# Order of one DMA queue in a fused tower kernel: item loads ahead of the Gram stores, and the Z result stored in one DMA

## The reference

```python
h = tok(x, embeddings)
h = h + attn(layernorm(h), ...)
h = h + ffn(layernorm(h), ...)

# attn: k, q, v = short_conv(x @ W.T + b); k, q normalized per head; v = silu(v)
# b = beta * k;  v = beta * v;  then, chunk by chunk of each sequence and head:
T = jnp.tril(Bi @ KiT, k=-1)
inv = jnp.linalg.inv(eyeC + T)
Ui = inv @ (Vi - Bi @ W_t)
W_new = W_t + KiT @ Ui
...
O_i = Qi @ W_avg * a + Qi @ W_t * c + T_mat * (Qi @ KiT) @ Ui
```

## Time and profile before

| | |
|---|---|
| median of three executions | 1499.64 us |
| the profiled execution | 1499.78 us |
| its span, first to last instruction | 1498.0 us |
| TensorE clock, mean granted | 0.877 |
| first stage with items (186 to 576 us) | 390 us, DVE busy 293, PE 238 |
| DMA share in that stretch | 0.73 |
| second stage with items (576 to 800 us) | 224 us, DMA share 0.80, then 0.76 |

### The profile page before, as it was taken

How to read it: one execution, slowest core, us unless ns; L and a number is a source line. 1 busy time by engine, 2 the same in 40 slices (tenths; PEclk the granted TensorE clock), 3 DMA queues, 4 the chain that set the end, 5 groups by cost and what they waited for, 6 DMA issues and landing times. The chain is left out here.

```text
span 1498.0 us, 28824 instructions
## 1 busy us (share of the span) xinstructions
PE 1181.4 (79%) x10846; PEld 795.5 (53%) x10846; DVE 762.3 (51%) x1707; ACT 516.6 (34%) x1049; POOL 390.3 (26%) x366
## 2 busy tenths in 40 slices
PE   4855465666666564787688988999999999999997
PEld 2643344353535352566466764665566666666664
DVE  4699959586868685478547873122111121111111
ACT  3454245453636261234152323331122222222221
POOL 6100123131112021533136004661022222222222
PEclk9878778787888785578788988999999999999999
DMA  7754557768695869688687748952122232323222
GB/s 265 195 125 125 129 165 171 225 149 245 136 255 120 253 134 267 200 244 246 172 256 230 222 129 338 346 167 78 28 47 47 45 48 43 47 47 46 47 46 30
DMA packets 237366, 228.68 MB, mean 153 GB/s; under 512 B 88980, under 2 KB 177972, under 8 KB 236080
## 3 DMA queue, kind: packets, MB, share of 16 engines
q1 hardware_dynamic: 202944, 194.28, 45.8%
q0 software_dynamic: 16368, 19.96, 7.7%
q10 hardware_dynamic: 17920, 12.59, 2.8%
HBM read 117.39 MB, written 115.62 MB: 156 GB/s over the span
## 5 line engine op out<-in xcount | busy, mean ns | idle before, releaser
L1683 DVE TENSOR_TENSOR hid_all<-p_s,silu 128x512 f32<-128x512 f32 x103 | 71.2, 691 | 379.4 <-PE p_s L1534 249.7
L1733 POOL DMA_INDIRECT out_h<-y_sb,x_in x71 | 110.5, 1557 | 360.9 <-DVE y_sb L1695 338.4
L1591 ACT ACTIVATE silu<-p_m 128x512 f32<-128x512 f32 x103 | 61.6, 598 | 328.0 <-PE p_m L1527 223.3
L801 DVE SCALAR_TENSOR_TENSOR cv<-raw,conv_sb,cv 128x512 f32<-128x512 f32 x144 | 116.5, 814 | 84.6 <-ACT raw L696 83.6
L172 DVE TENSOR_TENSOR prod<-nx,xt 128x62 f32<-128x62 f32 (+15 forms) x248 | 139.3, 562 | 2.5
L175 DVE TENSOR_TENSOR xt<-xt,prod 128x62 f32<-128x62 f32 (+15 forms) x248 | 138.4, 558 | 4.3
L290 PE MATMUL p_item<-xbd,bv_i 128*32 128x128 f32 x1024 | 48.1, 347 | 110.5 <-DMA xbd<-chunk_inverse_dram 37.6
L1549 PE MATMUL p_y<-wo,hid_all 128*128 x568 | 134.4, 379 | 0.8 <-ACT hid_all L1608 0.8
L1527 PE MATMUL p_m<-wi,xT_c 128*128 x284 | 133.6, 592 | 0.5 <-ACT xT_c L1604 0.5
L1534 PE MATMUL p_s<-ws,xT_c 128*128 x284 | 133.6, 593 | 0.0
L574 PE MATMUL p_p<-xT,wqkv_sb 128*128 128x512 f32 x192 | 108.7, 706 | 0.7 <-ACT xT L688 0.7
(11 more groups left out here) (155 smaller groups left out, 2124.4 us busy)
## 6 DMA issues: line engine op xcount, KB each, us to landing
slots_in_dram<-xt SPq DMA_DIRECT2D x18, 520.0 KB, 5.5
x_in<-slots_in_dram SPq DMA_DIRECT2D x71, 130.0 KB, 2.1
q_channels_dram<-qT SPq DMA_DIRECT2D x128, 64.0 KB
k_tokens_dram<-h SPq DMA_DIRECT2D x32, 256.0 KB
chunk_gram_dram<-h SPq DMA_DIRECT2D x32, 256.0 KB, 4.4
beta_kv_dram<-h SPq DMA_DIRECT2D x8, 1024.0 KB
nx<-chunk_gram_dram SPq DMA_DIRECT2D x8, 1024.0 KB, 6.3
scores_dram<-h SPq DMA_DIRECT2D x8, 1024.0 KB
```

What stands on the lines that cost most here:

```text
L801: ins = dve.scalar_tensor_tensor(cv[:, p, m, :], raw[:, p, m, j:j + L], conv_sb[:, p, m, j:j + 1], cv[:, p, m, :], ALU.mult, ALU.add)
L1683: dve.tensor_tensor(dst, p_s[n % 2][:], silu[n % 2][:], ALU.mult).then_inc(S["hid_ready"], 1)
L1733: pool.indirect_dma_start(token_rows, bass.IndirectOffsetOnAxis(x_in[s % X_IN][:, D:D + 1].bitcast(U32), 0), y_sb[s % 2][:], None, compute ...
```

## The change

Three things are edited, all in SP's list and what counts its DMAs. No arithmetic changes, and the lists of PE, DVE, ACT and POOL have the same instructions in the same order.

1. The Z tile of an item goes out in one DMA of 256 KB instead of four of 64 KB. Its semaphore counts follow.
2. In the passes 3 to 7, `load_x`, `store_y` and `store_rest` for the next item stand ahead of the first Gram stores instead of behind the `bv` store, and the scores load behind the first half of the Gram stores. After the second half, in passes 2 to 6, `load_x` and `store_y` for the next but one item come ahead of the wait for the Gram stores and of `nx`. In pass 2, item 0 is loaded ahead of the Gram stores instead of at the pass's end.
3. The store of beta k/v moves from between the halves of the Gram stores to behind `nx`, next to the scores store.

```diff
-            for c in range(CH):
-                sp.dma_start(zo_dram[t * CH + c, b], zo_out[i][tok(c)].rearrange("p w h d -> p (w h d)")
-                             ).then_inc(s_zo_st[i], 16)
+            sp.dma_start(zo_dram[t * CH:(t + 1) * CH, b], zo_out[i][:].rearrange("p w h d -> p (w h d)")).then_inc(s_zo_st[i], 16)
...
                     if b >= AHEAD:
-                        move_item(sp, r)
+                        if r:
+                            store_rest(sp, r - 1)
+                        load_scores(sp, r + 1)
                         move_item(sp, r + 1)
...
                                      kk[tok(c)].rearrange("p t h w d -> p t (h w d)")).then_inc(s_kst, 16)
+                    if b == AHEAD - 1:
+                        load_x(sp, 0)
+                        load_scores(sp, 0)
+                    if b >= AHEAD:
+                        load_x(sp, r + 4)
+                        store_y(sp, r + 3)
+                        store_rest(sp, r + 2)
                     for half in range(2):
...
-                        if half == 0:
-                            sp.wait_ge(s_bv, b * 4 + 4)
-                            sp.dma_start(bv_dram[b].rearrange("(t p) x -> p t x", p=P),
-                                         bv[:].rearrange("p t h w d -> p t (h w d)")).then_inc(s_st, 16)
-                            if b >= AHEAD:
-                                move_item(sp, r + 3)
+                        if half == 0 and b >= AHEAD:
+                            load_scores(sp, r + 4)
+                    if AHEAD - 1 <= b < B - 1:
+                        load_x(sp, r + 5)
+                        store_y(sp, r + 4)
                     sp.wait_ge(s_ngst, 64 * (b + 1))
                     sp.dma_start(nx[b % 2][:].rearrange("p i g j -> p (i g j)"),
                                  n_dram[b].rearrange("g (c i) x -> (g c) (i x)", i=C)).then_inc(s_nx, 16)
+                    sp.wait_ge(s_bv, b * 4 + 4)
+                    sp.dma_start(bv_dram[b].rearrange("(t p) x -> p t x", p=P),
+                                 bv[:].rearrange("p t h w d -> p t (h w d)")).then_inc(s_st, 16)
                     sp.wait_ge(s_sT, b * TILES + TILES)
                     sp.dma_start(sT_dram[b].rearrange("(t p) x -> p t x", p=P),
                                  sT[:].rearrange("p t g x -> p t (g x)")).then_inc(s_st, 16)
-                    if b == AHEAD - 1:
-                        load_x(sp, 0)
-                        load_scores(sp, 0)
```

More of the change, by code:

```diff
@@ L340, in turned_out @@
             if r >= 2:
-                act.wait_ge(s_zo_st[r % 2], 16 * CH * (r // 2))
+                act.wait_ge(s_zo_st[r % 2], 16 * (r // 2))
             act.copy(zo_out[r % 2][:, 0], bank[:].rearrange("p (h w d) -> p h w d", w=2, d=DH)[:, :, 1, :]).then_inc(T["z_ready"], 1)
@@ L975, in load_step @@
                     sp.wait_ge(s_y_st[t % 2], 16 * done)
-                    sp.wait_ge(s_zo_st[t % 2], 16 * CH * done)
+                    sp.wait_ge(s_zo_st[t % 2], 16 * done)
                     sp.wait_ge(s_qy_st[t % 2], 16 * done)
```

## The result

The changed kernel is slower. Over nineteen executions of each it took 1511.52 us against 1501.56 us, a ratio of 1.0072 with a 95% interval of 1.0052 to 1.0091. A later series of both gave 1.0083 (1.0057 to 1.0108). The forecast was 1480 us, and 1462 to 1502 us as its range; the measured time lies outside, on the other side of the kernel before. The profiled execution took 1501.8 us and is the fastest of the nineteen, while that of before lies 1.8 us under its median.

A forecast was written before the change was run, and what follows sets the result against it. No engine is full in the first stage; passes wait on SP's queued loads. Gains of 25.3 us there, less 1.5 into and 4 in the second stage, give 19.8 us off 1499.78: 1480 us, range 1462 to 1502.

The forecast's parts named there:

- the sum: Whole kernel: 25.3 us gained in the first stage, less 1.5 into and 4 in the second, 19.8 us in all.
- What bounds the kernel, and what comes late next: First stage: no engine full, passes wait on queued loads; after the change item 1's scores input `sbd` is late next.
- Pass 3: First pass with items: item 0 loaded some 18 us earlier, item 1's `sbd` lands at 198.2 against 212.14, gain 13.9 us.
- Passes 4 to 7: First stage: item 1's scores start earlier, by 3.5 us in pass 4, 2.2 in pass 6, 2.85 each in 5 and 7.
- in between SP issues item 1's xbd, bv_i and Y, 2.9 us ... hidden in that wait. nx leaves at 426.2, 1.9 us earlier than before: Start of pass 6: these loads' issuing fits inside the wait for the Gram's second half to land, so `nx` leaves earlier.
- issue of nx + 2.9 + MB behind it x 3.24: DMA queue: a load lands 2.9 us latency plus 3.24 us for each MB queued from `nx` on, after `nx` is issued.
- From there to DVE's last projection and the norms the order is unchanged, so the gain reaches the next pass: Behind item 1's scores in pass 6: PE and ACT keep their order, so the 2.2 us gain is passed on.
- The price of the narrow store: Z in one DMA runs on four engines: 2.4 us more for each store, SP saving 1.2 us of issuing.
- Into the second stage and through it: Item 21 starts 1.5 us later, 12 Z stores cost 4 us; later weight and Z loads cost nothing, 5 us if uncovered.
- The Z stores stand in the path: Rival, both stages: if 23 of 32 Z stores delay something waited for, 20 us slower, 1520 us; chance 0.10.

The follow-up runs named there:

- changed, again: The changed kernel, unaltered, run and traced a second time on the chip of the later runs; 1.0083 of the kernel before, trace span 1508.3 us.
- order_only: The changed kernel with Z in four stores again, so only edits 2 and 3 (the moves) stay; 0.9895 of the kernel before.
- pad_idle: Edits 2 and 3 with four Z stores, plus eight DMAs of 8 KB where SP was idle, in passes 3 to 7; 0.9919 of the kernel before.
- pad_nx: Edits 2 and 3 with four Z stores, plus eight DMAs of 8 KB ahead of `nx` in passes 2 to 6; 1.0013 of the kernel before.
- z_only: The kernel before with only edit 1, Z stored in one DMA, nothing moved; 1.0128 of the kernel before.
- scores_first: Edits 2 and 3, four Z stores, and item 1's scores inputs with the Z and queries stores moved right behind `nx`; 0.9791 of the kernel before.
- before_again: The kernel before, unchanged, traced again on the chip of later runs; 1504.45 us.
- z_spread: The changed kernel with its one Z store sent to 128 consecutive rows (128x512 on both sides, output not the reference's); 0.9858 of the kernel before.
- z_late: Edits 2 and 3, Z in four stores for the first stage's 20 items and one store for the second's 12; 0.9914 of the kernel before.

## Why the prediction was wrong

I take a pass apart in three stretches, each from starts and ends in the timelines: from DVE's last Gram write (L866, L872 in the changed kernel) to the issue of `nx`; from there to the scores of item 1; from there to the next last Gram write. Means over the four steps from pass 3 to pass 7, in us (for the step into pass 6 of the kernel before: 421.88, 428.05, 445.92). The row of the forecast is that of before less what the sum takes off in passes 4 to 7, 2.35 us ahead of `nx` and 0.5 behind it in the mean:

| | Gram to nx | nx to scores | scores to Gram | a pass |
|---|---|---|---|---|
| before | 8.2 | 18.2 | 51.6 | 78.0 |
| forecast | 5.9 | 17.7 | 51.6 | 75.2 |
| changed | 9.0 | 18.0 | 52.8 | 79.7 |
| changed, again | 9.2 | 17.8 | 52.8 | 79.8 |
| the moves alone (order_only) | 7.2 | 16.3 | 53.5 | 77.0 |
| pad_idle | 6.7 | 16.9 | 53.4 | 77.0 |
| pad_nx | 12.3 | 14.8 | 52.7 | 79.8 |
| z_only | 10.7 | 18.3 | 51.7 | 80.6 |
| scores_first | 6.2 | 10.8 | 55.9 | 72.9 |

- **What bounds the kernel, and what comes late next: right.** Item 0 and item 1 get their inverses in time, PE waits for `sbd` of item 1, ACT for the Z store. Scores_first, which moves both forward, shows that these were the waits to look at, and not which of the two.
- **Pass 3: 13.9 us forecast, 14.0 in the first trace** (212.14 to 198.11), 9.9 in the second and 10.0 in pad_idle, and 9.1 in order_only against before_again. Right in mechanism. The 14.0 is in part luck: two traces of the changed kernel differ by 4 us here, and no run shows by what.
- **Passes 4 to 7: 11.4 us forecast, 6.9 us lost.** Here the prediction failed. Of the 4.5 us a pass that it is off (79.7 less 75.2), 3.1 lie before `nx`, 0.3 between `nx` and the scores, 1.2 behind.
- **The failed step is "in between SP issues item 1's xbd, bv_i and Y, 2.9 us ... hidden in that wait. nx leaves at 426.2, 1.9 us earlier than before".** I had SP free at 421.5 us, 0.4 us before the Gram's second half was ready. In the trace it was free 3.5 us after (410.77 against 407.25), since it came to the k store 1.6 us later against the Gram write and since `sbd` and `q_i` took 5.1 us to issue, where the sum had 3.1. Then `xbd`, `bv_i` and Y took 4.9 us, not 2.9, longer than the 3.2 us of the Gram's landing that were to hide them: nothing was hidden, and `nx` left at 416.74, 9.5 us behind the Gram write, where the sum had 4.3. SP's issuing had no pause of even 1 us from the q stores to the Gram's second half, before as after: I read its single lengths and not that it was a bound of its own. Pad_nx and pad_idle show this: 5.6 us more before `nx`, of which 2.1 came back behind it (16.9 to 14.8) and 0.7 behind the scores; 2.8 us a pass stayed.
- **"issue of nx + 2.9 + MB behind it x 3.24": right where nothing was issued just ahead of `nx`.** For item 21 it gives 584.41 + 2.9 + 11.3 = 598.6, measured 598.56; likewise 602.3 in the second trace, 596.4 in order_only and 589.0 in pad_idle, measured 602.28, 596.39 and 589.05. In passes 4 to 7 it gave 15.05 us with four stores, and 14.8 was measured in pad_nx, but 16.3 and 16.9 in order_only and pad_idle: there 0.75 MB (`xbd`, `bv_i`, Y) had been issued just ahead of `nx`, which the formula doesn't count. That these bytes were still in the queue is the likely reason. With the narrow store it gave 17.5, and 16.7 to 19.5 was measured (mean 18.0). That this came so near is luck: the same 0.75 MB stands ahead there, and the store adds 1.7 us to the stretch against order_only (0.9 in the later pair), not the 2.4 of the sum.
- **"From there to DVE's last projection and the norms the order is unchanged, so the gain reaches the next pass": nearly.** This stretch grew by 1.2 us, by 1.9 with the moves alone, and by 4.3 in scores_first. The earlier start is not passed on whole. DVE has the same work to do in a shorter pass, which may be why; no run tests it.
- **The price of the narrow store: the shape was judged rightly, the size at half.** I had 9.7 us in passes 4 to 7 and 4 us behind, 13.7 together; the runs have 19 us alone and 25 to 27 on the moved order (1.0083 against 0.9919 and 1.0072 against 0.9895). I priced it as later landing of what stands behind. It also slows SP: behind a Z store, `sbd` took 4.04 us to issue in z_only and 1.98 in before_again, and the stretch before `nx` is 10.7 us in z_only where before_again has 7.9. That is the larger part in the first stage: between the moves alone and the changed kernel the difference is 1.8 and 2.5 us a pass before `nx`, in the two pairs of traces, and 1.7 and 0.9 behind it.
- **Into the second stage and through it: 5.5 us lost forecast, 9.8 and 13.2 measured** (from item 17's scores at 524.16, 517.00 and 521.45 to the chain's first piece). Pad_idle loses 6.2 without a narrow store. The weight and Z loads that I cost at nothing with 5 us at stake are one possible place. SP's issuing of four Z stores an item is another: z_spread, with one wide store, loses only 1.3 us there. No run isolates either.
- **The rivals.** "The Z stores stand in the path" was given 0.10 and came nearest. Its counting (23 of 32 stores with 2.4 us each) was not tested; the price that the runs show is 27 / 32 = 0.8 us a store on average.

In all: 33.5 us for the moves were 16, 13.7 for the store were 27, so 19.8 us of gain became 11 of loss.

Still open: how the store's price is split (the traces of the changed kernel again and pad_idle say 11 and 7 us, z_late's ratio 3 us for the second stage with up to 9 allowed, z_only's trace 17), which of item 1's scores and the Z store holds the passes after the moves, and why the stretch behind the scores grows as the pass shrinks.

## What to carry to other kernels

Where one engine issues all DMAs, read its issuing rows as a timeline of their own: if they are back to back ahead of a transfer that is waited for, each DMA moved in front of it delays it by its issuing time, however few bytes it has (5.6 us here for eight DMAs of 8 KB, of which 2.8 stayed in the pass). Then find what is late next and put that first: the scores' input and the Z store behind `nx` gave as much again (16 us) as all the moves before them. Don't merge DMAs into one whose first dimension is short; merge them so that both sides begin with a long one.

## What the runs showed of the hardware that I had not expected

- DMAs took longer to issue where many bytes were queued in front of them. Four DMAs of `sbd` took 1.93 and 2.72 us to issue in pass 6 before, and 9.32 us in the changed kernel, behind three transfers of 1 MB and a narrow Z store. With Z in four stores they still took 6.39 us there (order_only). What in the queue holds the issue is not shown.
- A store of 256 KB whose shape begins with 4 holds up the queue behind it (the queries store landed in 8.1 us, median, and not 2.9) and cost 0.8 us of the kernel's time each; as two stores that begin with 2 it cost twice that.
- Merging four DMAs into one that begins with 128 gave 0.4% by the medians over four DMAs of 32 rows, which can't be told from nothing (0.9858 and 0.9895, their intervals overlap).
